# Gamma and beta of a normalisation to GpSimd, a copy to VectorE, and unconditional waits in attention

## The reference

```python
# layer 0: gated linear attention (chunks of 64), then
x = _layernorm(x + _L0_attn_ref(x, ...), axis=-1)
# the mixture of experts normalises once more, with gamma and beta
mu = jnp.mean(xt, axis=-1, keepdims=True)
var = jnp.mean(jnp.square(xt - mu), axis=-1, keepdims=True)
normed = (xt - mu) * jax.lax.rsqrt(var + LN_EPS) * ln_gamma + ln_beta
logits = normed.astype(jnp.float32) @ router_w.T
...
# layer 1: differential attention, 16 heads of 16, causal, two softmaxes a head
s1 = jnp.einsum('bhqd,bhkd->bhqk', q1, k1) * scale
s2 = jnp.einsum('bhqd,bhkd->bhqk', q2, k2) * scale
...
attn = a1 - lam.astype(dtype)[None, :, None, None] * a2
out = jnp.einsum('bhqk,bhkd->bhqd', attn, v)
```

## Time and profile before

| | before |
|---|---|
| time, median of 3 runs | 2308.34 us (2306.82 to 2311.7) |
| profiled execution: its time, its span | 2308.34 us, 2306.6 us |
| TensorE busy (matmuls) | 2145.9 us, 93% |
| VectorE busy | 1579.9 us, 68% |
| ScalarE busy | 1240.6 us, 54% |
| GpSimd busy | 634.4 us, 28% |
| layer 0's attention | about 0 to 362 us, steps of 44.2 us |
| layer 1's attention | about 1235 to 2085 us |

### The profile page before, as it was taken

The page is one execution under the profiler, slowest core; times in us unless marked ns, Lnnn a source line. Parts: engine busy times, 40 slices in busy tenths (PEclk is TensorE's granted clock), DMA queues, the critical chain, the costliest instruction groups (busy, mean ns, idle before and its releaser), DMA issues.

```text
span 2306.6 us, 47108 instructions
## 1 busy us (share of the span) xinstructions
PE 2145.9 (93%) x17816; PEld 1324.1 (57%) x17816; DVE 1579.9 (68%) x2712; ACT 1240.6 (54%) x2379; POOL 634.4 (28%) x749
## 2 busy tenths in 40 slices
PE   7999999789999999985875899999999999999998
PEld 5888886456666666654653333334334334347886
DVE  4677666633333333337989999989989998926878
ACT  5767664213333333223331699888888889863110
POOL 1000000103333333333556133433343243222000
PEclk9999999999999999997986799999999999999999
DMA  4333325652222222223333011002002001200000
GB/s 140 129 120 120 120 88 203 203 198 34 54 37 35 38 38 38 36 38 138 138 132 122 27 52 41 32 31 61 32 30 61 33 30 43 71 20 1 28 19 28
DMA packets 90027, 163.77 MB, mean 71 GB/s; under 512 B 16224, under 2 KB 64352, under 8 KB 88144
## 3 DMA queue, kind: packets, MB, share of 16 engines
q1 hardware_dynamic: 76176, 141.98, 18.0%
q0 software_dynamic: 13632, 18.77, 5.1%
HBM read 99.70 MB, written 60.49 MB: 69 GB/s over the span
## 4 chain that ended last, share of the span: by engine, by line
PE 54%; DVE 18%; ACT 2%; issue 2%; DMA 1%; SPq 1%; POOL 0%; DVEq 0%; ACTq 0%
DVE NM L2154 11%; PE PS L1446 8%; PE PS L2271 8%; PE PS L58 7%; PE PS L60 6%; PE PS L59 6%; PE PS L2353 6%; PE PS L2296 3%; PE PS L1431 2%; DVE TT L1639 2%; PE PS L2224 1%; DVE X L2545 1%; PE PS L2291 1%; PE PS L2317 1%; ACT E L2057 1%
## 5 line engine op out<-in xcount | busy, mean ns | idle before, releaser
L2154 DVE TENSOR_REDUCE NM<-PS 128x2 f32<-128x1024 f32 (+3 forms) x608 | 673.7, 1164 | 55.8 <-PE PS L2296 52.2
L2057 ACT ACTIVATE E<-PS 128x512 f32<-128x512 f32 (+2 forms) x1280 | 625.4, 556 | 90.3 <-PE PS L2353 73.8
L2271 PE MATMUL PS<-E,VP 128*32 128x256 f32 (+1 forms) x5120 | 363.9, 370 | 5.9 <-ACT OT L2091 2.3
L1243 DVE SCALAR_TENSOR_TENSOR XIL<-PS,XSC,XIH 128x128 f16<-128x128 f32 x142 | 43.3, 347 | 336.1 <-ACT XIH L1039 336.1
L1991 POOL TENSOR_SCALAR_AFFINE_SELECT E<-E 128x512 f32<-128x512 f32 x256 | 163.2, 638 | 375.0 <-ACT E L2057 373.9
L1074 ACT ACTIVATE HB<-PS 128x768 f32<-128x768 f32 x71 | 57.5, 810 | 300.9 <-PE PS L1431 300.9
L2271 PEld LDWEIGHTS PS<-E,VP 128*32 128x32 f32 x5120 | 111.1, 108 | 184.5 <-issue 96.8
L2353 PE MATMUL PS<-QK 50*128 50x512 f16 (+3 forms) x1152 | 195.1, 333 | 6.1 <-ACT E L2057 4.0
L1446 PE MATMUL PS<-WALL,HB 128*128 x852 | 195.7, 379 | 1.0 <-ACT HB L1074 1.0
L2296 PE MATMUL PS<-QK 48*128 48x512 f16 (+3 forms) x1152 | 185.9, 342 | 6.3 <-DVE NM L2154 6.2
L983 POOL DMA_INDIRECT XB<-x_normed,IDX x71 | 70.9, 999 | 365.0 <-DVE GAT L1259 316.7
(11 more groups left out here) (352 smaller groups left out, 3936.7 us busy)
## 6 DMA issues: line engine op xcount, KB each, us to landing
parts<-PP SPq DMA_DIRECT2D x32, 512.0 KB, 3.0
WIN<-in_we SPq DMA_DIRECT2D x16, 768.0 KB, 5.2
QK<-parts SPq DMA_DIRECT2D x96, 128.0 KB
WALL<-pairs_of_weights SPq DMA_DIRECT2D x7, 1536.0 KB
pairs_of_weights<-WPH SPq DMA_DIRECT2D x16, 384.0 KB, 2.4
pairs_of_weights<-WPL SPq DMA_DIRECT2D x16, 384.0 KB, 3.3
WALL<-in_we SPq DMA_DIRECT2D x8, 768.0 KB
QK<-parts SPq DMA_DIRECT2D x96, 64.0 KB
```

The lines of the kernel that those rows point to most:

```text
L2057: e.activation(dst, src, ACT.Exp, scale=unit).then_inc(S.ex, 1)
L2154: e.tensor_reduce(dst, src, AX, ALU.max).then_inc(S.mx, 1)
L2271: a = e.matmul(PS[32 * jj:32 * jj + 32, 7, 512 - n + c0:512 - n + c1], VP[b % 2][:, kt, 17 * hd:17 * hd + 32], E[:, m % NE, jj, c0:c1], st ...
```

## The change

In `gla`:
- The second normalisation on VectorE becomes four plain instructions into nav (subtract the mean, multiply by the root; `layernorm_apply`, L86), and they raise a new semaphore `n2`. GpSimd then multiplies all of nav's block by gamma and adds beta, two instructions of 128x1024, and raises `nr`. In step 8 GpSimd does this for the first two tiles and VectorE for the last two.
- The low part of the next x (XTL) moves from behind the state updates to just behind the four instructions.
- The copy of NTT moves from ScalarE to VectorE, behind the state updates, in all steps.
- SP's reload of XS waits for `n2` instead of `nr`. Where all eight blocks are waited for, `nr` must reach 9.

In `attention`, the waits that stood only at the first reader now stand at every one: ScalarE's for `pe_av` at each exponential, TensorE's for `vp_ld` at the first half of each product block, for `qk_ld` at each maximum, for `row_ld` at each score matmul.

```diff
@@ sp, gla
-                    e.wait_ge(S.nr, u + 1)
+                    e.wait_ge(S.n2, u + 1)
                     e.dma_start(XS[u % 2][:], x_in[:, :, u + 2, :]).then_inc(xs_ld[u % 2], 16)
-                e.wait_ge(S.nr, u + 1)
+                e.wait_ge(S.nr, u + 1 + (u == 7))
@@ pool, gla (behind the products L219)
+            if t > 0:
+                e.wait_ge(S.n2, u + 1)
+                if u == 0:
+                    e.wait_ge(S.g_ld_out, 64)
+                nb = 4 if t < 8 else 2
+                n = own.pool.on(e.tensor_tensor(nav[:, 0:nb, u, :], nav[:, 0:nb, u, :], GAM[:].unsqueeze(1).to_broadcast([128, nb, 256]), ALU.mult))
+                e.wait_ge(own.pool.sem, n)
+                e.tensor_tensor(nav[:, 0:nb, u, :], nav[:, 0:nb, u, :], BET[:].unsqueeze(1).to_broadcast([128, nb, 256]), ALU.add).then_inc(S.nr, 1)
@@ act, gla
-                if t > 0:
-                    for k in HALF:
-                        e.wait_ge(S.pe_nt, 2 * u + k + 1)
-                        if u > 0:
-                            e.wait_ge(S.pe_x1, u + 2)
-                        e.activation(NTT[:, k], rows(PS[:, out_banks(t)[2][k], :]), ACT.Copy).then_inc(S.ntt, 1)
@@ dve, gla
-                if u == 0:
-                    e.wait_ge(S.g_ld_out, 64)
-                for b in QUAD:
-                    n = own.dve.on(e.scalar_tensor_tensor(out=nav[:, b, u, :], in0=xu[b], scalar=K.MV[:, b, 0:1], in1=GAM[:], op0=ALU.subtract, op1=ALU.mult))
-                for b in QUAD:
-                    e.wait_ge(own.dve.sem, n - 3 + b)
-                    a = e.scalar_tensor_tensor(out=nav[:, b, u, :], in0=nav[:, b, u, :], scalar=K.RS[:, b:b + 1], in1=BET[:], op0=ALU.mult, op1=ALU.add)
-                a.then_inc(S.nr, 1)
+                layernorm_apply(e, K, xu, [nav[:, b, u, :] for b in QUAD])[-1].then_inc(S.n2, 1)
+            if t < 7:
+                e.wait_ge(S.xhi, t + 2)
+                e.tensor_tensor(XTL[:], XTS[(t + 1) % 2][:], XTH[:].bitcast(F32), ALU.subtract).then_inc(S.xlo, 1)
...
-                    e.wait_ge(S.pe_lg, u)
+                    if u > 0:
+                        e.wait_ge(S.pe_lg, u)
                     e.tensor_copy(NTT[:, k], rows(PS[:, nt_bank[k], :])).then_inc(S.ntt, 1)
...
-                if t < 7:
-                    e.wait_ge(S.xhi, t + 2)
-                    e.tensor_tensor(XTL[:], XTS[(t + 1) % 2][:], XTH[:].bitcast(F32), ALU.subtract).then_inc(S.xlo, 1)
+                if t > 0:
+                    turn_out()
...
             else:
+                e.wait_ge(S.n2, u + 1)
+                own.dve.on(e.tensor_tensor(nav[:, 2:4, u, :], nav[:, 2:4, u, :], GAM[:].unsqueeze(1).to_broadcast([128, 2, 256]), ALU.mult))
+                e.wait_ge(own.dve.sem, own.dve.n)
+                e.tensor_tensor(nav[:, 2:4, u, :], nav[:, 2:4, u, :], BET[:].unsqueeze(1).to_broadcast([128, 2, 256]), ALU.add).then_inc(S.nr, 1)
@@ done, gla
-        e.wait_ge(S.nr, 8)
+        e.wait_ge(S.nr, 9)
@@ act, attention, exponentials
-                if m >= NE and i == exps_to(m):
+                if m >= NE:
                     e.wait_ge(S.pe_av, m - NE + 1)
@@ pe, attention, products
-                if g == 0 and m % 12 == 0:
-                    e.wait_ge(vp_ld[b % 2], 16 * (b // 2 + 1))
+                e.wait_ge(vp_ld[b % 2], 16 * (b // 2 + 1))
@@ pe, attention, maximum
-            if u == 0:
-                e.wait_ge(qk_ld[v % 4], 128 * (v // 4 + 1))
+            e.wait_ge(qk_ld[v % 4], 128 * (v // 4 + 1))
@@ pe, attention, scores
-                    if s == 0 and y == 0 and x == 0:
-                        e.wait_ge(row_ld[w % 4], 64 * (w // 4 + 1))
+                    e.wait_ge(row_ld[w % 4], 64 * (w // 4 + 1))
```

More of the change, by code:

```diff
@@ L92 @@
     g_ws g_wst wphi wplo
-    xhi xlo whi wlo xg ga gg vv yt ep em qg kd kg at kz sga wor ss sq sm sr yy xa mv rs nr ntt lg""")
+    xhi xlo whi wlo xg ga gg vv yt ep em qg kd kg at kz sga wor ss sq sm sr yy xa mv rs n2 nr ntt lg""")
 def gla(nc, A, K, PS, D, own):
```

## The result

The changed kernel takes 2337.12 us in the median of 4 runs (2335.39 to 2339.7), the kernel before on the same occasion 2307.58 us (2305.76 to 2311.7). The ratio is 1.0125, with a 95% interval of 1.0108 to 1.0140: 25 to 32 us slower. The profiled execution of the changed kernel took 2334.71 us with a span of 2333.0, which is 26.4 us over the span before. So the forecast of 2329 named the right side. The measured median lies in the stated range of 2315 to 2342, just above the forecast's own 2322 to 2336. The forecast difference of 20.7 us was 6 us (spans, 26.4) to 9 us (medians, 29.5) too low. These few microseconds are what the rest is about.

The account below looks back on a forecast made before the run. TensorE was taken as the bound, busy nearly throughout, with VectorE close in layer 1's attention. Stall 13.9, clock 4.8 and waits 2 sum to 20.7 us over 2308.34: 2329.0 us, range 2315 to 2342, forecast's own 2322 to 2336.

Parts of the forecast that it names:

- TensorE's stall: Layer 0's attention: rows ready after 6.92 us, wanted after 4.94, so TensorE waits 1.98 us in seven iterations, 13.9 us.
- half clock behind it: Layer 0's attention: three of seven pauses followed by a half-clock stretch of 3.2 us, 1.6 us each, 4.8 us.
- waits in layer 1: Layer 1's attention: about 2400 added TensorE waits, 122 us of sequencer, almost all hidden under the array; 2 us shows.
- GpSimd's price: Layer 0's attention: each 128x1024 product on GpSimd takes 2.20 us, bounds 2.12 and 2.25.
- The hold-up: Layer 0's attention: the low part of x on VectorE lengthens GpSimd's first product by 0.93 us, bounds 0 and 1.22.
- the handoffs: Layer 0's attention: three handoffs between the plain instructions, GpSimd's two products and the transposes, 0.07 us each.
- The rival of exposed waits: Layer 1's attention: a tenth or more of the new waits exposed, 12 us beside 18.7, 2339 or more; chance 0.13.
- Costed at nothing: Layer 0's attention: NTT copies on VectorE, the moved low part, SP's reload and the last iteration add no time.
- The rival of a mild stall: Layer 0's attention: GpSimd not held up, pauses too short for the clock, 6.2 to 9 us with waits, 2316; chance 0.15.
- the case of no loss: Layer 0's attention: GpSimd's products take 1.67 us each or less, TensorE gets no wait, at most 2.8 us won; chance 0.10.

Follow-up runs that it names:

- experiment 9: The kernel before, with the low part of x ahead of the state updates in step 0 alone: 2307.25 us, ratio 0.9991.
- experiment 2: The changed kernel with the low part of x back behind the state updates: 2323.51 us, ratio 1.0051.
- experiment 6: Changed kernel, no added layer-1 waits, gamma and beta split between GpSimd and VectorE every step, copies ahead of low part: 2317.61 us, ratio 1.0032.
- layer 0 only: The changed kernel with layer 1's attention as before, without the added waits: 2331.84 us, ratio 1.0096.
- experiment 7: The kernel before with the added waits of layer 1's attention, TensorE's three each written three times: 2332.46 us, ratio 1.0101.
- experiment 5: The kernel before with NTT copies on VectorE and low part ahead of state updates: 2313.58 us, ratio 1.0022; copies alone: 2316.58 us, ratio 1.0030.
- experiment 3: The changed kernel with GpSimd's addition of beta left out: 2309.22 us, ratio 0.9990.

## Why the prediction was right, and where its sizes were off

The mechanism in layer 0 was the forecast one, place by place; the sizes were not, and a term that no step of the prediction had makes up most of what the sum lacked. Term by term, from the two profiles:

| term | forecast, us | measured, us | from |
|---|---|---|---|
| TensorE's stall | 7 x 1.98 = 13.9 | 6 x 2.21 + 1.29 = 14.6 | idle before L686 in steps 1 to 6 and in step 7 |
| half clock behind it | 3 x 1.6 = 4.8 | 5 x 1.43 = 7.2 | steps of 47.90 against 46.47 with the pause filled |
| first step | 0 | -1.15 | experiment 9 |
| waits in layer 1 | 2 | 1.3 | 801.3 against 800.0 |
| behind layer 1's attention | 0 | 4.8 | 227.8 against 223.0 |
| sum | 20.7 | 26.7 | spans: 26.4 |

**The stall.** GpSimd's price was too low: 2.34 to 2.36 us for 1024 elements and not 2.20, which is also over the upper bound of 2.25 that I took from half of 2048 elements. The hold-up was 0.92 us where 0.93 stood. Together 5.62 + 1.38 and the handoffs make 7.2 us, of which 4.94 were free. In step 7 there is no low part, hence no hold-up and 1.29 us only; I had counted seven equal steps, and the two errors nearly cancel.
The hold-up came under L452 and went with it: the first product takes 3.28 us beside it, 2.36 in experiment 2 and in step 7. The sum let the second product run beside VectorE's state updates without a hold-up, and the trace of before has no such pair; the product takes 2.34 us there, with or without L452. The prediction let only GpSimd be held up. In the changed kernel that was so, L452 kept its 1.22 us; experiment 6 shows VectorE held up as well, 1.65 us for 0.69, where its product started second.

**The clock.** This is the term of the sum that was most mis-sized: three of seven stretches, from five comparable pauses in the trace of before: a stretch at 0.50, of 3.4 us by its clock record, stands behind those at 362.9, 2041.8 and 2114.6 us, none behind those at 30.3 and 432.6. There were five, behind five of six pauses of 2.2 us, in three traces at the same places (the changed kernel twice, and layer 0 only); none behind the pauses of 1.30 us of experiment 2. Each cost 1.4 us and not 1.6 in the first profile, where TensorE still waits at its start (busy 2.94 of 3.30 us in the row above); in the repeat, where the clock falls only behind the pause, each cost 1.5. Why the first pause of 2.2 us passes without one was not settled.

**The waits.** The rival of exposed waits is out: the share was 1.3 us of 122, about 1 us less the clock's part. The argument was right, though thinner than it sounded, as experiment 7 shows: a second instruction at each place cost 22 us. That each added wait is one more sequencer instruction was my inference from L2283 alone. Single waits bear it out, 2397 more in this stage for the 2400 reckoned; waits written three times do not, two more at a place.

**Costed at nothing.** Right in the sum, wrong as a statement about the moves: without the rest of the change the copies cost 1.13 us a step, and with the low part moved too it is 1.14 (experiment 5); here both are covered by the 1.9 us that the plain normalisation frees on VectorE. I had named the cover of the copies (3.75 us between the transposes and the reader of NTT) but not that of the low part, and the state updates behind it are on TensorE's path. In step 0, which has no normalisation, the low part ahead of the updates wins 1.15 us; the prediction had no such term. SP and ScalarE were nothing in the steady steps, as the 44.2 us of experiment 3 show, and ahead of step 8's transposes TensorE does not wait.

**The last part.** No step of the prediction had it, and no part of the change touches its code. These 4.8 us are most of the 5.7 that lie between the forecast sum and the two profiles, and they are the clock of that stage: 7.4 us lost to it in the changed kernel's trace, 2.7 in that of before. Without them the measured terms add up to 22.0 us for the forecast 20.7, and that nearness is in part luck: the 2.4 us that the clock term lacked are mostly made up by the first step's 1.15 and by the 0.7 that the waits had too much. In the late stages one kernel did not always get the same falls: the two traces of the changed kernel have 227.8 and 229.1 us behind attentions of 801.3 and 806.6, and the kernel before spread over 12 us on one occasion. Against a purely random pattern stand the two traces of the kernel before, alike within 0.1 us in both stages, and layer 0, where five of the same six pauses had a fall in all three traces.

What stays open: the median difference of 29.5 us is 3 us above that of the two profiled spans, and 6 us above the sum of the two halves measured apart (21.4 and 2.1). The intervals overlap (25 to 32; 18 to 27 and -1 to 5), so that may be only the scatter of this clock; whether a later start of the last stages makes the worse pattern more frequent was not tried.

The rival of a mild stall is out (no pause below 2.20 us in steps 1 to 6); the case of no loss asked for 1.67 us a product of 1024 elements, and the shortest took 2.34. The 2.8 us that this case could have won are TensorE's idle time in the earlier trace rows, 280.00 - 277.17.

## What to carry to other kernels

Before work is moved to a relieved engine, measure the time from its first instruction to the first reader on the engine that bounds the stage; here 4.94 us were free and 7.2 were needed, and the load taken from VectorE and ScalarE bought nothing, since TensorE was the bound. An instruction slipped in on the old engine lengthened the one on the new engine here (2.36 to 3.28 us) and the other way round (0.69 to 1.65 us), so price the pair, not the instruction, and look which of the two starts first. And a pause of the bounding engine had a second price in its clock, 1.4 us behind five of six pauses of 2.2 us; filling the pause with useless matmuls gave back about a quarter of the whole loss (a ratio of 1.0089 for 1.0125). Single profiles differ by several microseconds through the clock in stages that no edit touched (219.6 to 221.0 us of the last part without it, 221 to 229 with it): compare by stage, and take that part out first.

## What the runs showed of the hardware beyond what was expected

- GpSimd and VectorE held each other up, and in the rows of experiment 6 the one that started second paid: VectorE's 128x512 product took 0.69 us where it started 0.04 us ahead of GpSimd's (which took 1.78 for 1.06), and 1.64 to 1.79 where GpSimd's had started first.
- Of otherwise equal pauses of TensorE, those of 2.2 us had a stretch at 0.50 behind them in five of six cases, the same five in three traces; those of 1.3 us in experiment 2 in none of seven.
- One added wait at each matmul group of this stage cost at most 0.6 ns of the time, a second one 9 ns, at 51 ns of sequencer time each; TensorE looked busier with them (809.71 of 823.30 us, against 781.68 of 800.00), so lost issue time did not show as idle time.
- Two executions of the changed kernel differed by 9 us, of which 6.6 lie in layer 1's attention and the last part, by their clock.
